# First attention: the values of the compressed branch as four products of 32 rows side by side

## The reference

```python
entries = jnp.einsum('bcr,bcrh->bch', w_cmp, hidden_states.reshape(Bq, C, RATIO, HID))
ck = apply_rope(rmsnorm(entries @ Wk + bk, kn_w), block_ends)
cv = entries @ Wv + bv
sc = jnp.einsum('bhsd,bcd->bhsc', q, ck) * scale          # then masked, top 8, softmax
...
ctx_sparse = jnp.einsum('bhsk,bhskd->bhsd', pw, v_g)      # v_g: rows of cv, the same for all heads
ctx_local = jnp.einsum('bhcqk,bhckd->bhcqd', pl, vw).reshape(Bq, NH, Sq, D)
merged = (ctx_sparse + ctx_local) * 0.5
out = merged.transpose(0, 2, 1, 3).reshape(Bq, Sq, NH * D) @ Wo + bo
```

## Time and profile before

| | us |
|---|---|
| median of the 2 runs shown | 2750.59 (2749.55 to 2751.62) |
| the profiled execution | 2741.3 |
| its span, first to last instruction | 2739.5 |
| PE busy in the span | 2321.4 (85%) |
| DVE busy | 1870.4 (68%) |
| ACT busy | 1589.4 (58%) |
| GpSimd busy | 714.6 (26%) |

### The profile page before, as it was taken

The page is one execution under the profiler, slowest core; times in us unless marked ns, Lnnn a source line. Parts: engine busy times, 40 slices in busy tenths (PEclk is TensorE's granted clock), DMA queues, the critical chain, the costliest instruction groups (busy, mean ns, idle before and its releaser), DMA issues. The chain is left out here.

```text
span 2739.5 us, 50448 instructions
## 1 busy us (share of the span) xinstructions
PE 2321.4 (85%) x16399; PEld 1526.4 (56%) x16545; DVE 1870.4 (68%) x4371; ACT 1589.4 (58%) x3099; POOL 714.6 (26%) x897
## 2 busy tenths in 40 slices
PE   6999999999987567777777689889997986899994
PEld 3676766767664334444444445545555664467773
DVE  5777778777775989999999912256665775234443
ACT  3656666566664679999989911056664654223332
POOL 1121121211210122222222200011111267336664
PEclk9999999999999799999989989999998998899997
DMA  5000000000001599999999920140000022446666
GB/s 199 1 1 0 0 0 0 0 0 0 0 0 47 97 200 189 184 178 188 176 175 191 185 55 1 35 114 1 1 1 7 13 68 79 140 89 109 108 111 142
DMA packets 539447, 211.18 MB, mean 77 GB/s; under 512 B 475002, under 2 KB 533878, under 8 KB 538230
## 3 DMA queue, kind: packets, MB, share of 16 engines
q1 hardware_dynamic: 518246, 180.54, 33.0%
q0 software_dynamic: 20592, 27.98, 5.9%
q10 hardware_dynamic: 416, 0.16, 0.0%
HBM read 54.27 MB, written 36.90 MB: 33 GB/s over the span
## 5 line engine op out<-in xcount | busy, mean ns | idle before, releaser
L1752 DVE TENSOR_SCALAR_CACHE_REDUCE x_row<-x_p_s,x_nsq 128x1024 f32<-128x1024 f32 x512 | 621.6, 1273 | 22.2 <-PE x_p_s L1527 21.8
L1631 ACT ACTIVATE x_ints<-x_row,x_nb 128x2048 uint16<-128x2048 f32 x256 | 511.7, 2000 | 50.9 <-DMA x_turned<-x_ints 32.7
L1527 PE MATMUL x_p_s<-x_kT,x_qz 128*128 128x512 bf16 x929 | 295.2, 406 | 150.2 <-DVE x_row L1752 142.2
L363 POOL TENSOR_TENSOR a_rstd<-a_ssq,neghalf 128x16 f32<-128x16 f32 x32 | 125.9, 3934 | 522.9 <-DVE a_ssq L874 522.9
L1527 PEld LDWEIGHTS x_p_s<-x_kT,x_qz 128*128 128x128 bf16 x1024 | 72.5, 101 | 270.7 <-DVE x_row L1752 246.0
L3276 POOL DMA_INDIRECT f_acc<-f_yt,f_ids x111 | 171.8, 1548 | 135.5 <-ACT f_yt L3441 117.4
L1655 POOL TENSOR_SCALAR x_nb<-x_low,x_hmin 128x1 f32<-128x1 f32 x256 | 74.4, 291 | 505.6 <-DVE x_row L1752 504.3
L1561 PEld LDWEIGHTS x_p_o<-x_vi,x_turned 128*128 128x128 f16 x4096 | 142.8, 97 | 87.1 <-DMA x_turned<-x_ints 19.3
L2215 ACT COPY s_eT<-sc_p_e 128x512 f32<-128x512 f32 x192 | 112.1, 584 | 133.9 <-PE sc_p_e L2105 133.8
L1561 PE MATMUL x_p_o<-x_vi,x_turned 128*128 128x16 bf16 x4096 | 142.3, 170 | 18.6 <-DMA x_turned<-x_ints 18.3
L2105 PE MATMUL sc_p_e<-ident,s_e 128*128 128x128 f32 x768 | 123.7, 285 | 33.0 <-ACT s_eT L2215 21.6
(11 more groups left out here) (479 smaller groups left out, 5314.5 us busy)
## 6 DMA issues: line engine op xcount, KB each, us to landing
f_rows<-f_spread SPq DMA_DIRECT2D x111, 136.5 KB, 2.1
f_w<-in_L_ffn_w_dram SPq DMA_DIRECT2D x2, 2816.0 KB
x_turned<-x_ints SPq DMA_TRANSPOSE x224, 4.8
f_sum<-f_acc SPq DMA_DIRECT2D x6, 512.0 KB, 7.6
f_w<-in_L_ffn_w_dram SPq DMA_DIRECT2D x2, 1408.0 KB
f_spread<-f_empty SPq DMA_DIRECT2D x17, 136.5 KB, 2.5
x_res<-in_x_dram SPq DMA_DIRECT2D x2, 1024.0 KB, 6.9
a_wq<-in_L_attn_Wq_dram SPq DMA_DIRECT2D x2, 1024.0 KB, 10.6
```

The source lines that it names most:

```text
L363: pool.tensor_tensor(rstd[:, hs], ssq[:, hs], core.neghalf[:, 0:NH], ALU.pow).then_inc(root_h.sem, 1)
L1527: mm = pe.matmul(p_s[n % SLOTS][:, c * BANK:(c + 1) * BANK], qz[b % 2][:, par, a, :], kT[:, a, at:at + BANK], start=True, stop=True)
L1631: act.activation(ints[k][:, :], rows[k][:, :, :].rearrange("p s n -> p (s n)"), ACT.Exp, bias=nb[:, k:k + 1], scale=-1.0, accum_out=esum[: ...
L1752: dve.tensor_scalar(rows[k][:, half, :], p_s[n % SLOTS][:, :], nsq[:, b % 2, h:h + 1], HIGHEST, ALU.mult, ALU.min, accum_out=(low if half ...
```

## The change

The compressed values of four heads of a group, which had been four products of 128 rows with three quarters zeros, become part of four wider products, one per group: 32 rows (the entries) of `cv`, held once over 128 partitions, with 512 columns (four heads by 128 tokens). The four read different partitions and write four different banks, `context` = `p_cT`, `p_pT`, `work[0]`, `work[1]`; the local products of `values0` to `values3` then accumulate onto them. To make 32 rows of `psT` hold the four heads of a group, the scores are formed from adjacent heads (`qT[:, j * NG:(j + 1) * NG, :]`), and the multiplication by the query scales on DVE reads the scales in a matching order. ACT copies `cv` once. PE and ACT get new orders, and the waits follow the banks.

```diff
-        cv = sb("a0_cv", [P, G, D])
+        cv = sb("a0_cv", [P, D])
...
+        context = (p_cT, p_pT, work[0], work[1])
...
-            pool.memset(cv[:, :, :], 0.0).then_inc(cleared, 1)
...
@@ turn_heads, for the first two of a batch
-                        pe.wait_ge(l_exp.sem, l_exp.of(b - 1, NG - 1 + n))
+                        pe.wait_ge(cT_read.sem, cT_read.of(b - 1, NG - 1 + n))
@@ sparse_scores
-                                   qT[:, j::G, :], start=True, stop=True)
+                                   qT[:, j * NG:(j + 1) * NG, :], start=True, stop=True)
@@ turn_prob
+                    if g in (0, 2):
+                        pe.wait_ge(cT_read.sem, cT_read.of(b, g))
...
+            def sparse_values(b):
+                pe.wait_ge(proj_read.sem, proj_read.of(b))
+                pe.wait_ge(c_read.sem, c_read.of(b))
+                pe.wait_ge(cT_read.sem, cT_read.of(b, 0))
+                pe.wait_ge(pT_read.sem, pT_read.of(b, 2))
+                pe.wait_ge(l_exp.sem, l_exp.of(b))
+                for g in range(NG):
+                    rows_of = slice(g * NC, (g + 1) * NC)
+                    pe.matmul(context[g][:, :], cv[rows_of, :], psT[rows_of, :, :].rearrange("p j t -> p (j t)"), start=True, stop=False)
+
             def values(g):
                 def run(b):
                     pe.wait_ge(pT_read.sem, pT_read.of(b, g + 1))
-                    pe.wait_ge(cT_read.sem, cT_read.of(b, g))
-                    if g == 0:
-                        pe.wait_ge(proj_read.sem, proj_read.of(b))
-                        pe.wait_ge(c_read.sem, c_read.of(b))
                     for h in range(G):
-                        o = p_cT[:, h * P:(h + 1) * P]
                         at = (g * G + h) * D
-                        pe.matmul(o, raw[2][:, at:at + D], pT[g % 2][:, h, :], start=(h == 0), stop=False)
-                        mm = pe.matmul(o, cv[:, h, :], psT[:, g, :], start=False, stop=(h == G - 1))
+                        mm = pe.matmul(context[g][:, h * P:(h + 1) * P], raw[2][:, at:at + D], pT[g % 2][:, h, :],
+                                       start=False, stop=(h == G - 1))
                     mm.then_inc(cT_made.sem, 1)
@@ PE's order, from s3 on
-                     ("s3", 1), ("turn_sparse", 1), ("k2", 0), ("values0", 1), ("turn_p1", 1), ("k3", 0), ("turn_p2", 1),
-                     ("entries", 0), ("values1", 1), ("out0", 1), ("values2", 1), ("turn_p3", 1), ("out1", 1),
-                     ("values3", 1), ("comp_kv", 0), ("v0", 0), ("v1", 0), ("v2", 0), ("v3", 0), ("out2", 1),
+                     ("s3", 1), ("turn_sparse", 1), ("k2", 0), ("turn_p1", 1), ("k3", 0), ("sparse_values", 1), ("values0", 1),
+                     ("values1", 1), ("entries", 0), ("out0", 1), ("turn_p2", 1), ("out1", 1), ("turn_p3", 1), ("values2", 1),
+                     ("comp_kv", 0), ("values3", 1), ("v0", 0), ("v1", 0), ("v2", 0), ("v3", 0), ("out2", 1),
                      ("comp_key", 0)], pieces, B, before=1)
@@ ACT: compressed_up
-                for h in range(G):
-                    q = slice(NC * h, NC * (h + 1))
-                    last = act.copy(cv[q, h, :], bank[q, D:2 * D])
-                last.then_inc(proj_read.sem, 1)
+                act.copy(cv[:, :], bank[:, D:2 * D]).then_inc(proj_read.sem, 1)
@@ ACT: context_up
-                    act.copy(cT[g % 2][:, :, :].rearrange("p g t -> p (g t)"), p_cT[:, :]).then_inc(cT_read.sem, 1)
+                    act.copy(cT[g % 2][:, :, :].rearrange("p g t -> p (g t)"), context[g][:, :]).then_inc(cT_read.sem, 1)
@@ ACT's order, from square_q on
-                      ("square_q", 0), ("turn_sparse", 1), ("exp2", 1), ("turn_p1", 1), ("values0", 1), ("exp3", 1),
-                      ("turn_p2", 1), ("values1", 1), ("values2", 1), ("turn_p3", 1), ("entries", 0), ("square_k", 0),
-                      ("comp_kv", 0), ("v0", 0), ("v1", 0), ("v2", 0), ("v3", 0), ("values3", 1)], pieces, B, before=1)
+                      ("square_q", 0), ("turn_sparse", 1), ("exp2", 1), ("turn_p1", 1), ("exp3", 1), ("values0", 1),
+                      ("values1", 1), ("entries", 0), ("turn_p2", 1), ("turn_p3", 1), ("values2", 1), ("square_k", 0),
+                      ("comp_kv", 0), ("v0", 0), ("v1", 0), ("values3", 1), ("v2", 0), ("v3", 0)], pieces, B, before=1)
@@ DVE: sparse_arg
-                dve.tensor_tensor(scm[:, :, :], scm[:, :, :], bcast(rqs[:, :], [P, NH, NC]), ALU.mult).then_inc(s_arg.sem, 1)
+                placed = scm[:, :, :].rearrange("p (m g) c -> p m g c", g=NG)
+                scales = rqs[:, :].rearrange("p (g m) -> p m g", m=G).unsqueeze(3).to_broadcast([P, G, NG, NC])
+                dve.tensor_tensor(placed, placed, scales, ALU.mult).then_inc(s_arg.sem, 1)
```

More of the change, by code:

```diff
@@ L575, in _ @@
             pieces = {"in": turn_in, "entries": entries, "comp_kv": compressed_kv, "comp_key": compressed_key,
-                      "sparse": sparse_scores, "sparse_back": sparse_back, "turn_sparse": turn_sparse}
+                      "sparse": sparse_scores, "sparse_back": sparse_back, "turn_sparse": turn_sparse, "sparse_values": sparse_values}
             for g in range(NG):
@@ L658, in compressed_up @@
                 act.copy(ckr[:, :], bank[:, 0:D])
-                if isinstance(b, int) and b == 0:
-                    act.wait_ge(cleared, 1)
-                for h in range(G):
-                    q = slice(NC * h, NC * (h + 1))
-                    last = act.copy(cv[q, h, :], bank[q, D:2 * D])
-                last.then_inc(proj_read.sem, 1)
+                act.copy(cv[:, :], bank[:, D:2 * D]).then_inc(proj_read.sem, 1)
             def compressed_key_up(b):
```

## The result

The changed kernel takes 2832.56 us (median of 2 runs, 2830.36 to 2834.76) against 2750.59, which is 82.0 more. The measured ratio is 1.028 [1.0244 to 1.0316]; the two medians alone would give 1.030. The direction of the forecast holds; its size does not, the median lies 20 us above the top of the range. The profiled execution took 2830.36 us; its span is 89.1 us longer than before.

What follows compares the result with a forecast made beforehand. First attention bound by PE's own order of work, 16 batches of 49.05 us. Per batch -2.55 + 3.2 + 1.2 = +1.85, times 16 = +30; clock +12; 2741.3 + 42 = 2783, plus 9.3 for the median: 2793 us, range 2768 to 2813.

Steps and rivals of the forecast that it cites:

- The saving: PE, first attention: four compressed shares (3.62 us) become one group of four products (1.07), saving 2.55 a batch, 41 in all.
- The serial rival: PE: the four products don't run side by side, 2.37 us a batch more, giving 2831; chance 0.04.
- The stall: PE ahead of the four products: all four banks wait for `exp3`, a stall of 3.2 us in each batch.
- the two rivals in which the wait shrinks or vanishes: PE's wait for `exp3`: stall only 1.4, giving 2751, chance 0.07; or covered, giving 2729 or 2710, chance 0.07.
- The wait for `comp_key`: PE waits 1.2 us a batch because ACT's `square_k` stands behind the copy of `values2`; ends 0 and 1.2.
- The clock: First attention's loop: half the batches pay 1.5 us for 3.4 us at half speed, 12 in all; ends 0 and 27.
- the prediction's signs: First attention's loop: if right, PE idles about 3.2 and 1.2 us, group takes 1.07, period near 51, clock sometimes 0.50.
- the rival with the clock in every batch: First attention's loop: every batch pays for the low clock, +30 + 27 us, giving 2808; chance 0.10.

Runs made afterwards that it cites:

- 1: Changed kernel plus three dummy products on PE ahead of the wait for the last exponentials; 1.0122 of the kernel before.
- 2: Changed kernel plus the three dummy products on PE, and `square_k` on ACT ahead of the copies of `turn_p3` and `values2`; 1.0054 of the kernel before.
- 5: Changed kernel with the four products in two pairs, only the second waiting for the last exponentials, behind `entries`; 1.0033 of the kernel before.
- 7: Changed kernel with the products in two pairs and `square_k` earlier on ACT; 0.9936 of the kernel before, 2737.36 us against 2754.79.
- 3: Changed kernel with `square_k` on ACT ahead of the copies of `turn_p3` and `values2`, no dummy products; 1.0131 of the kernel before.
- 4: Changed kernel plus one dummy product of 256 columns on PE in each batch, ahead of `turn_p2`; 1.0249 of the kernel before.
- 6: Kernel before, 128-row products kept, with `values0` behind `k3` waiting for `exp3`, and ACT's `exp3` ahead of the copy of `values0`; 1.026 of the kernel before.

## Why the prediction was wrong in size

**The saving: right.** It is 2.55 a batch; the group takes 1.07 at full clock (1, and the balance of 2). The serial rival gave 2831, nearly the measured number, by luck, for its reason does not hold: the 2.02 us of the group after are the low clock, not a serial array.

**The stall: right.** 3.2 forecast, 3.21 measured. `exp3` was held where the forecast held it: from `turn_p0` to its end 8.92 us (452.83 to 461.75), 8.99 before. With that the two rivals in which the wait shrinks or vanishes fall.

**The wait for `comp_key`: there, but worth 1.67 and not 1.2**, 7.5 us in all. The row's idle of 0.99 is not its whole price: in 5 the next instruction starts 0.59 behind `comp_key` (504.14 to 504.73), in 7 after 0.11 (390.71 to 390.82), which is 0.48 more. Nearly all of the remaining 0.2 is overlap: in 7 `comp_key` starts 0.16 before the products ahead of it have ended.

**The clock: the step that failed.** "I take it that about half of the batches pay, each with 3.4 us at half speed, less what of it falls into the stall: 1.5 us, 12 us in all. The ends are 0 and 16 x 1.7 = 27." The runs put 43 us there (after against 1), some 46 by the mean clock of 0.94. Both factors were too small: the clock fell in all but one of the fifteen batches of the loop in which PE idled 3.05 us, not in half of them, and from 298 us on each of eleven falls in a row lasts 6.8 us, which is 3.19 a batch and not 1.5; so the period became 54.6, where the prediction's signs had near 51. The length of 6.8 stood in the earlier trace rows, in the stretch from 46.2 to 53.0; I put it down to the longer idle of 4.61 and took the 3.4 of the tail for mine, though no row said that an idle of 3.2 costs the shorter one. Experiments 3 and 4 show why that reading fails, and so does the changed kernel before it settles: the same idle of 3.05 is followed by 6.8 us, 3.4 or nothing. In this stretch of it PE resumes after that idle at 193.42:
```profile
144.20:246.40 102.20, 92.92 (x460) 60.25 (x459) 73.77 (x214) 58.93 (x162) 17.84 (x12) 1.00 0.00 0
```
With the measured terms the sum closes: 16 x (-2.55 + 3.2 + 1.67) + 43 = 80 us, and the first attention became 80.1 longer. In a settled batch it is -2.55 + 3.2 + 1.67 + 3.19 = 5.51, where the trace has 5.56.

So the rival with the clock in every batch was nearest, and its own price of 1.7 a batch was short by half. The Trainium skill (TensorE: Matmul & The Clock Gate, Why this matters for your kernels) warns against idle gaps between bursts of matmuls. The runs agree with it in the main: with an idle of 3.05 us the clock fell in fourteen of those fifteen batches, with PE kept busy through the same wait in none (1, 2).

**What stays open.** Why the changed kernel settles where every batch pays for 6.8 us, 3 where each pays for 3.4, and 4 in neither, was not settled. That the place of the fall against the resume matters is read from rows, not made: no run shifted the fall alone. Open too is why in 5 one batch of the loop paid after an idle of 0.99.

## What to carry to other kernels

When a change makes a busy engine wait once per pass of a loop, price the clock apart from the wait, by the longest low stretch that any row of the trace shows, and give the range that end in every pass. Before several products are put into one group, look for whose wait each of their banks brings along: here a wait needed by two of four banks held up all, and a split cost less than the wait, even though it gave up 1.05 us of the saving, and 0.33 beside it. Fill an unavoidable idle with dummy products if nothing better is at hand; here it gave back 1.6%.

## What the runs showed of the hardware

- One idle of PE of 3.04 to 3.05 us had three prices: none, about 1.6 us (3.4 at clock 0.50: 1.68 in 3, 1.53 in 6) or about 3 (6.8 at 0.50: 3.19 in the changed kernel; 54.72 - 51.95 = 2.77 in 4). What is lost is about half of the low time behind the resume: in 3 the clock falls with it (398.2, resume at 398.19) and is back after 3.4; in the changed kernel it falls before it (0.50 from 461.7 at the latest, resume at 461.90) and is low to 468.3 at least, 6.4 us behind the resume, half of which is 3.2.
- Waits are not additive under such a clock: 1.67 us of waiting taken out gave back 3.15 a batch (54.58 to 51.43).
- A fall needs no idle of 3 us: in 5 the clock stood at 0.50 for 3.3 us in one batch whose longest idle was 0.99.
- Two products of 32 rows and 512 columns side by side take 1.06 us, four take 1.07: half a group costs as much as a full one.
